# A transformer block on one core: query and key stacks filled within on-chip memory, with the work ahead of the attention loop in another order

## The reference

```python
n = layernorm(x); q, k, v = n @ Wq.T, n @ Wk.T, n @ Wv.T      # 256 x 256 each
q, k = rope(q), rope(k)                                       # halves of the 256 columns turned against each other
heads: 16 of 16
memory = elu1(k)^T v ; norm = sum(elu1(k))                    # the linear branch, per head
mem_out = elu1(q) memory / (elu1(q) norm)
attn = softmax(q k^T / 4) v                                   # per head, 1024 x 1024
x = x + (sigmoid(gate) * mem_out + (1 - sigmoid(gate)) * attn) @ Wo.T
x = x + moe(layernorm(x))       # 8 experts, hidden 688, silu(gate) * up, best 2 of 8 per token
```

## Time and profile before

| | |
|---|---|
| time, median of 3 runs | 445.03 us (442.81 to 445.61) |
| the profiled execution's own time | 448.04 us |
| its span in the profile | 446.1 us |
| busy PE / DVE / ACT / POOL | 405.4 / 267.7 / 198.2 / 98.2 us |
| mean granted clock of TensorE | 0.967 of full |
| HBM read / written | 30.05 / 18.74 MB |

### The profile page before, as it was taken

How to read it: one execution, slowest core, us unless ns; L and a number is a source line. 1 busy time by engine, 2 the same in 40 slices (tenths; PEclk the granted TensorE clock), 3 DMA queues, 4 the chain that set the end, 5 groups by cost and what they waited for, 6 DMA issues and landing times.

```text
span 446.1 us, 6508 instructions
## 1 busy us (share of the span) xinstructions
PE 405.4 (91%) x2144; PEld 202.0 (45%) x2145; DVE 267.7 (60%) x513; ACT 198.2 (44%) x349; POOL 98.2 (22%) x92
## 2 busy tenths in 40 slices
PE   0887799979999999999999799999999999999992
PEld 0526175222222232342332123577665677777771
DVE  6498899866888888779979610278233233233230
ACT  0236825756676766657656598411111111111110
POOL 6100660421011011001014220006421421212112
PEclk9998589998999999999989999999999999999997
DMA  6227674467264453203013169525422232211131
GB/s 201 106 71 141 108 176 95 121 209 240 97 206 148 162 190 113 63 1 129 0 39 138 49 232 337 160 72 186 84 37 37 40 44 37 35 36 25 24 107 24
DMA packets 24409, 48.15 MB, mean 108 GB/s; under 512 B 4448, under 2 KB 17888, under 8 KB 22528
## 3 DMA queue, kind: packets, MB, share of 16 engines
q0 software_dynamic: 7824, 30.27, 22.7%
q1 hardware_dynamic: 15984, 15.96, 14.4%
q10 hardware_dynamic: 576, 1.58, 1.1%
HBM read 30.05 MB, written 18.74 MB: 109 GB/s over the span
## 4 chain that ended last, share of the span: by engine, by line
PE 72%; DVE 12%; DMA 5%; issue 2%; ACT 2%; SPq 2%; another core or an unknown queue 2%; POOL 1%; DVEq 0%; POOLq 0%; ACTq 0%
PE psum L1227 66%; DVE mem L948 6%; PE psum L1491 2%; DMA parts_d<-mem 2%; DMA mem<-x 1%; ACT mem L778 1%; DMA mem<-mem 1%; PE psum L1351 1%; PE psum L1480 1%; SPq L432 1%; DVE mem L1013 1%; DMA out<-mem 1%; DVE mem L885 1%; POOL mem L539 1%
## 5 line engine op out<-in xcount | busy, mean ns | idle before, releaser
L1227 PE MATMUL psum<-mem 128*32 128x512 f32 (+10 forms) x1904 | 381.3, 461 | 18.6 <-DMA mem<-parts_d 2.8
L1227 PEld LDWEIGHTS psum<-mem 128*32 128x32 f32 (+4 forms) x1904 | 173.0, 134 | 205.0 <-issue 84.1
L948 DVE TENSOR_REDUCE mem<-psum 128x1 f32<-128x1024 f32 x128 | 152.1, 1219 | 33.3 <-PE psum L1227 30.3
L778 ACT ACTIVATE mem<-psum 128x512 f32<-128x512 f32 x256 | 137.3, 604 | 64.8 <-PE psum L1227 59.5
L792 ACT ACTIVATE mem<-psum 128x688 f32<-128x688 f32 x18 | 13.4, 746 | 85.6 <-PE psum L1227 79.4
L647 POOL DMA_INDIRECT sum_d<-mem x17 | 26.6, 1564 | 79.4 <-ACT mem L796 63.4
L1111 DVE COPY mem<-mem 128x3 f32<-128x3 f32 x18 | 3.0, 169 | 57.6 <-PE psum L1480 52.5
L1123 DVE COPY mem<-psum 128x512 f32<-128x512 f32 x18 | 12.5, 692 | 28.4 <-PE psum L1491 27.5
L796 ACT ACTIVATE mem<-psum,mem 128x256 f32<-128x256 f32 x18 | 8.5, 474 | 40.8 <-PE psum L1227 36.6
L599 POOL DMA_DIRECT2D mem<-gate_up x7 | 4.0, 572 | 75.8 <-DMA mem<-mem 75.8
L1115 DVE TENSOR_TENSOR mem<-mem,psum 128x688 f32<-128x688 f32 x18 | 15.7, 870 | 5.0 <-ACT mem L792 4.3
(11 more groups left out here) (121 smaller groups left out, 199.4 us busy)
## 6 DMA issues: line engine op xcount, KB each, us to landing
mem<-gate_up POOLq DMA_DIRECT2D x8, 1376.0 KB
xg_d<-mem POOLq DMA_DIRECT2D x8, 1036.0 KB, 5.9
mem<-down POOLq DMA_DIRECT2D x4, 1024.0 KB, 10.4
mem<-parts_d SPq DMA_DIRECT2D x24, 128.0 KB, 4.3
mem<-parts_d SPq DMA_DIRECT2D x48, 64.0 KB, 2.3
parts_d<-mem SPq DMA_DIRECT2D x18, 128.0 KB, 1.8
mem<-xg_d SPq DMA_DIRECT2D x16, 129.5 KB
mem<-down POOLq DMA_DIRECT2D x2, 704.0 KB, 12.6
```

The source lines that it names most:

```text
L778: nc.scalar.activation(prob[:, t % 8], psum[:, score_bank(n, t)], ACT.Exp, scale=HD ** -0.5).then_inc(exp_ready, 1)
L948: V.tensor_reduce(mx[:, par, k:k + 1], banks(2 * (k % 2), 2), AX.X, ALU.max).then_inc(max_ready, 1)
L1227: return nc.tensor.matmul(*a, **k)
```

## The change

- **Stacks from SBUF.** DRAM's `parts_d` goes. `k_group` and `q_group` copy 64 partitions (a quad of a block) straight to the 16 rows of a group, four heads wide. For this a partition's place within a quad must be r * 4 + j in place of j * 16 + r: ScalarE reorders the columns of Wk and Wq into `w_turned` ahead of the projections, and the tables of cosine and sine and the mask of the state are reordered in the constants. The linear branch runs in the new order, with the same counts.
- **SP's order.** `first_stacks(i)` for i = 0, 1, 2 issues six 64 KB copies, each group as soon as its part is there (keys in two halves of the tokens). Then stacks(1), a wait for the low parts of block 1, stacks(2), max_rows(0, 0), stacks(3), a wait for the parts of i = 3, max_rows(1, 1). `stacks` now holds its key stack too, waits until that has landed, and issues the query stack. The loop over u is written out.
- **Block 1's splits.** GpSimd does the rotations of block 1 for the queries (i = 2, 3) and the residuals and low parts of block 1; VectorE keeps the keys' rotations.
- **Order on ScalarE.** v_copy 0 and 1 go between the high parts of block 1, v_copy 2 and 3 behind the exponential of k; hi_part(3) goes behind the copies of the turned kfeat.
- **Values between scores.** Four value tiles stay ahead of the scores, the others follow steps 3, 5, 7 and 9. lin_turn moves to steps 23 to 26, lin_state to steps 31 to 34.
- **Clears.** Fills 0 to 2 are issued on GpSimd right after the first norm, ahead of all the rest; fills 3 and 4, then 5, 6, 7 and the last one stand behind gate_up 0, 1, 2 and 3, which wait for the rows of maxima of the next unit, as before.

```diff
+            def quad_rows(w, part, qd, c):
+                p = qd % 2 * 4 * HD
+                return parts[p:p + 4 * HD, w, part, qd // 2, c]
+            def k_group(g, qd, c, done):
+                sp.dma_start(kst[g * HD:(g + 1) * HD, qd, :, c], quad_rows(0, KPART[g], qd, c)).then_inc(done, 16)
+            def q_group(g, qd, hf, sl):
+                sp.dma_start(qst[g * HD:(g + 1) * HD, sl], quad_rows(1, QPART[g], qd, cols(hf))).then_inc(q_in, 16)
+            def first_stacks(i):
+                for part, ready in enumerate((hi_ready, mid_ready, lo_ready)):
+                    sp.wait_ge(ready[0], i + 1)
+                    for g in range(GROUPS):
+                        if i < 2 and KPART[g] == part:
+                            k_group(g, 0, cols(i), k0_in)
+                        if i == 2 and QPART[g] == part:
+                            q_group(g, 0, 0, 0)
...
             def stacks(qd):
+                k_stack(qd)
                 sp.wait_ge(k_in, 16 * GROUPS * qd)
                 sp.wait_ge(q_in, 16 * GROUPS * qd)
                 q_stack(qd, 0, qd)
...
-            k_stack(1, k_in)
+            for i in range(3):
+                first_stacks(i)
             stacks(1)
-            for i in range(3):
-                parts_out_1(i)
-            for i in range(3):
-                sp.wait_ge(part_out_1[i], 48)
-            k_stack(2, k_in)
+            sp.wait_ge(lo_ready[1], 3)
+            stacks(2)
             max_rows(0, 0)
-            stacks(2)
-            k_stack(3, k_in)
             stacks(3)
-            parts_out(3)
-            for s in range(3):
-                sp.wait_ge(part_out[3][s], 16)
+            sp.wait_ge(lo_ready[2], 1)
             max_rows(1, 1)
...
+            pool.wait_ge(xg_set, 1)
+            for e in range(3):
+                fill(e * T, (e + 1) * T)
+            for i in (2, 3):
+                w, hf = QK_IDX[i]
+                m = (tmp, tmp_odd)[i % 2]
+                pool.wait_ge(rope_mul, i + 1)
+                nc.gpsimd.tensor_tensor(qT[:, 1, cols(hf)], m[:, 2], m[:, 3], ALU.add).then_inc(rope_q1, 1)
+            pool.wait_ge(lo_ready[0], 2)
+            for i in range(3):
+                w, hf = QK_IDX[i]
+                pool.wait_ge(hi_ready[1], i + 1)
+                nc.gpsimd.tensor_tensor(RESID_1[i], (kT, qT)[w][:, 1, cols(hf)], parts[:, w, 0, 1, cols(hf)],
+                                        ALU.subtract).then_inc(res_ready[1], 1)
+            for i in range(3):
+                w, hf = QK_IDX[i]
+                pool.wait_ge(mid_ready[1], i + 1)
+                nc.gpsimd.tensor_tensor(parts[:, w, 2, 1, cols(hf)], RESID_1[i], parts[:, w, 1, 1, cols(hf)],
+                                        ALU.subtract).then_inc(lo_ready[1], 1)
...
+            FILLS = [(3, 4), (5,), (6,), (7,)]
+            for u in range(NQ):
+                load_gate_up(u)
+                for e in FILLS[u]:
+                    fill(e * T, (e + 1) * T)
+                if u == NQ - 1:
+                    fill(E * T, NSLOT)
+                pool.wait_ge(av_ps, 8 * u + 8)
+                stage_v(u + 2, u % 2, (u + 2) % NQ)
             load_gate_up(NQ)
...
+            for w in range(2):
+                act.wait_ge(w_in[w], 16)
+                nc.scalar.copy(w_turned[:, w].rearrange("p b (q r j) -> p (b q) j r", r=HD, j=4),
+                               wqkv[:, w].rearrange("p b (q j r) -> p (b q) j r", j=4, r=HD)).then_inc(w_turned_ready, 1)
...
-            for n in range(TT):
+            for n in range(4):
+                values(n)
...
-                if s in (17, 19, 21, 23):
-                    lin_turn((s - 17) // 4, (s - 17) // 2 % 2)
-                if s in (25, 27, 29, 31):
-                    lin_state((s - 25) // 4, (s - 25) // 2 % 2)
+                if s in (3, 5, 7, 9):
+                    values(4 + (s - 3) // 2)
+                if s in (23, 24, 25, 26):
+                    lin_turn((s - 23) // 2, (s - 23) % 2)
+                if s in (31, 32, 33, 34):
+                    lin_state((s - 31) // 2, (s - 31) % 2)
```

More of the change, by code:

```diff
@@ L129, in block_kernel @@
         qst = words(A + 8192, 4, 4, HALF, dt=BF16)
+        w_turned = words(A + 11264, 2, HB, H)
         max_ones = mem[SROWS:SROWS + 2, A:A + 2 * NQ * T]
@@ L395, in _ @@
             sp.dma_start(router, router_d).then_inc(router_in, 16)
[L397 to L415, removed]
-                for g in range(GROUPS):
-                    src = parts_d[0, KPART[g]].rearrange("(q j r) t -> q r j t", j=4, r=HD)[qd]
-                    sp.dma_start(kst[g * HD:(g + 1) * HD, qd], src).then_inc(done, 16)
@@ L426, in max_rows, with k_stack, q_stack @@
+            def k_stack(qd):
+                for g in range(GROUPS):
+                    k_group(g, qd, slice(0, T), k_in)
+            def q_stack(qd, hf, sl):
+                for g in range(GROUPS):
+                    q_group(g, qd, hf, sl)
             def max_rows(u, sl):
@@ L549, in stage_v, with fill @@
                 nc.gpsimd.tensor_copy(vst[:, sl, :, :, 0:HD], src).then_inc(v_staged, 1)
+            def fill(lo, hi):
+                pool.dma_start(xg_d[lo:hi].rearrange("(n p) h -> p n h", p=P),
+                               xn2[:, 0, 0:1].to_broadcast([P, (hi - lo) // P, ROW])).then_inc(xg_filled, 16)
+            pool.wait_ge(xg_set, 1)
[17 more added lines that the diff above has]
+                                        ALU.subtract).then_inc(lo_ready[1], 1)
             pool.wait_ge(v_ready, 4)
@@ L724, in _ @@
             for i in range(3):
-                act.wait_ge(rope_1, i + 1)
+                act.wait_ge(rope_q1, 1) if i == 2 else act.wait_ge(rope_k1, i + 1)
                 hi_part(i, 1).then_inc(hi_ready[1], 1)
-            v_copy(0)
-            v_copy(1)
+                if i:
+                    v_copy(i - 1)
             act.wait_ge(rope_mul, 4)
@@ L738, in _ @@
             nc.scalar.activation(exp_k, exp_k, ACT.Exp, scale=-1.0).then_inc(nexp_ready, 1)
-            act.wait_ge(rope_1, 4)
+            v_copy(2)
+            v_copy(3)
+            act.wait_ge(rope_0, 4)
+            act.wait_ge(rope_q1, 2)
             nc.scalar.activation(qfeat, qT, ACT.Relu).then_inc(relu_ready, 1)
@@ L785, in steps @@
                         turned_copy(hf, k)
+            act.wait_ge(lo_ready[1], 3)
             attention(act, steps)
@@ L934, in _ @@
             turns(3, 1).then_inc(rope_mul, 1)
-            other(3)
-            for i in range(3):
-                rest(i, 1)
-            for i in range(3):
-                low_part(i, 1)
             def score_side(i, t):
@@ L1247, in _, with values @@
             pe.wait_ge(w_in[2], 16)
-            pe.wait_ge(xnT_ready, 4)
-            for n in range(TT):
+            def values(n):
                 if n % 4 == 0:
```

97 lines of the change are left out of this document (29 added, 68 removed).

## The result

The changed kernel takes 439.76 us (median of 4 runs, 439.47 to 440.68), the kernel before 444.86 (4 runs, 442.81 to 445.61): ratio 0.9904, 95% interval 0.9874 to 0.9934, faster by 5.1 us. The forecast was 439.8. The profiled execution took 439.96 us, its span is 438.1, the mean granted clock 0.981.

The account below looks back on a forecast made before the run. TensorE, busy 91%, was taken to set the time in the long middle and at the end. 1.2 us at the loop's start plus 4.0 for the hole made 5.2, from a median of 445.03 to 439.8; range 435.5 to 444.5.

Parts of the forecast that it names:

- The sum: Whole kernel: 1.2 us won at the loop's start plus 4.0 from the hole, 5.2 us in all, giving 439.8 us.
- The first stacks: Before the scores: DRAM writes and their waits go, so the first score comes at 39.5, 6.2 us earlier.
- The lead, up to the turns: Scores before the first lin_turn: later value tiles cost nothing, pair 11 is done at 54.5, kfeat is ready at 54.6.
- GpSimd's new work is hidden under ScalarE: In the lead: GpSimd's rotations, residuals and low parts end near 46.4, before v_ready, with over 2 us to spare.
- The turns cost part of the win: Four lin_turns after steps 23 to 26, at half clock: VectorE idles, and 3.3 of the 6.2 us are left.
- The states cost another part: lin_state after steps 31 to 34: VectorE waits from 63.9 to 65.9 with the mask; 1.2 us reach the loop.
- Little is kept: Rival: kfeat late, so nothing won at the mask, or the hole stays in part; 2 us faster, 443, chance 0.18.
- The queue of SP: Before the loop: stacks(2) goes ahead of max_rows(0,0); at 131 GB/s SP is free with 6 us of slack.
- the slower rival: On-chip copies below 60 GB/s make SP block the maxima; at 50 GB/s the kernel takes 455 us; chance 0.08.
- The hole in the loop: Unit 1's rows of maxima: with no fills beside them TensorE's 2.27 us wait goes, plus 1.7 of half-rate clock, 4.0.

Follow-up runs that it names:

- its one essential part alone: The kernel before with only its stacks filled directly from SBUF in SP's new order, all else as before: 442.62 us, ratio 0.9859.
- the last experiment: The changed kernel with GpSimd's first scatter moved behind its wait for the last scores: 452.94 us against 444.16 for the kernel before, ratio 1.0204.

## Why the prediction was right

**The sum.** 5.2 us were forecast, 1.2 at the start and 4.0 for the hole, and 5.1 measured on the first chip. The traces give 0.14 and 4.04 to these terms, 4.2 us. That the total came within 0.1 us is in part luck: the kernel before had late waits in its trace which no term names, and the changed one had none. On the third chip the same kernel gained 2.5 us (0.9925, 0.99 to 0.9949). This interval overlaps that of 0.9904, but the forecast's ratio, 0.988, lies outside it; why it was 2.5 and not 4.2 stays open, as the kernel before has no trace there.

**The first stacks: right.** The first score waits for TensorE's values; the first maximum came at 40.48 against 40.2, pair 11 was done at 54.50 against 54.5. The start as a whole stood 0.54 us later: the first rotation began at 21.25 and not 20.71, because the clock rose at 18.80 and not 17.76 and the projections ahead of it ran longer at half rate. VectorE's last multiplication ended at 39.88 and not at 38.2 (0.54 of it from there, 1.07 from L898 beside GpSimd): with 0.60 us of idle time ahead of the first maximum it was near to deciding.

**The lead, up to the turns: chain right, one hand-over missed.** kfeat was forecast at 54.6 and came at 55.66. The step "GpSimd's new work is hidden under ScalarE" failed: two of ScalarE's three middle parts wait 0.50 us each for a residual of GpSimd's 1.13, so exp_k's first half started at 45.14 and not about 43.7 (0.4 of it is the later start). The prediction compared when GpSimd's work ends, and not its pace with ScalarE's. GpSimd's operations were sized rightly (L556 and L561, 3.39 for three, 1.13 each). The copies of the weights take 2.04 us for the two and not 1.2, and still hide: TensorE's second eight transposes start at 14.48, where they started at 14.42.

**The turns cost part of the win: right, and slightly larger.** VectorE idles 4.08 and 0.75 us, 3.8 were forecast; the clock was at half there, 49.52 to 59.76. The rows of maxima are sent at 64.72 against 63.9.

**The states cost another part: the mechanism was right, the size too large by 1.1.** The mask begins at 66.83 against 65.9; it was given 1.2 us to win, and the loop starts 0.14 earlier. Some 0.5 of the shortfall is the clock's rise at the start, the rest kfeat. The prediction's own bound, nothing won if kfeat comes 1.2 us later than worked out, and the rival *Little is kept* (kfeat late, nothing at the mask) named this case: kfeat came 1.06 later, and for the start of the loop it is what happened. The experiments turn the account round. Of the 6.3 us of the first maximum, 3 buy nothing, as a score 3 us later gives the same start; the others are worth some 2 at the loop, and kfeat, 2.8 us later than before (55.66 against 52.85), takes these back. I had kfeat ahead of the first turn, at 1.7 us later than before, but did not follow that all else ahead of it is slack then, and that a microsecond of kfeat is then nearly one of the loop's start (1.7 for 2.0).

**The queue of SP: right, with less to spare.** Key stack 1 ran at 114 GB/s with the DMA engines full. The windows of the changed kernel, 39 to 44 and 52 to 56 us (length, busy engines, clock, DMA share, GB/s):

```profile
39.00:44.00 5.00, 4.98 (x23) 3.33 (x23) 4.40 (x6) 3.46 (x4) 4.04 (x4) 0.97 0.94 114
52.00:56.00 4.00, 1.33 (x5) 0.42 (x5) 2.50 (x3) 3.47 (x2) 4.00 (x2) 0.50 0.98 112
```

This is under the 131 of the reads from DRAM, far over the 60 from which the slower rival decides, and SP issued the rows within 0.1 us of their being ready. It had stood 3.6 us for them, where 6 were forecast. The Trainium skill ("SBUF — State Buffer", Door 1: The DMA port swizzle) gives about 109 GB/s for 16 partitions; 112 and 114 lie near it. A source in SBUF at the same time took nothing off that figure, though it may be part of the step down from 131: no run separates them.

**The hole in the loop: size right, cause only half.** 4.0 forecast, 4.04 found between first exponential and first turn, with no half-rate stretch behind. (The rows were needed 23.1 us after the loop's start, 97.0 less 73.92, and not 23.4; nothing hangs on it.) But I gave it to the clears' move. The runs show that the direct stacks alone remove it as well, and that in the kernel before the fills stood at 89.05 because of the writes of parts. My step looked at what ran beside the rows and not at why it ran just then.

## What to carry to other kernels

When several edits feed one start, find which input arrives last there and delay each other input by a few microseconds: an input that can be 3 us later for nothing is not worth an edit. Run a large change also as its one essential part alone: here that part was faster than the whole, because the reordering around it lengthened the chain that set the start. Check a match of forecast and median term by term in the traces: here the total agreed to 0.1 us and one of its two terms was off by 1.1. Before a transfer is moved out of another's way, ask why it was issued at that moment.

## What the runs showed of the hardware

- **GpSimd against small VectorE operations.** Two-input VectorE operations on SBUF stood until a GpSimd one ended: 1.76 us and not 0.69 beside L551, 2.05 and not 0.17 beside L582. The Trainium skill ("SBUF — State Buffer", 🔬 SBUF: two separate sides) calls the shared port pair an exclusive lock also for VectorE operations with two SBUF inputs, against a GpSimd operation that reads SBUF; these rows agree. It goes both ways: L551 at 34.57 took 1.64 us, and 1.27 at 39.96; beside the first, VectorE's L914 ran until 35.08. The cast of 16 columns with one input took 0.40 and not 0.17. Not every such pair is held: two comparisons of 32 columns at 295.23 took 0.29 us beside a GpSimd power of 4 columns.
- **Issues of on-chip copies.** Six from SBUF to SBUF take SP 3.78 us, 0.63 each, the six reads from DRAM took 2.68, 0.45 each.
- **A copy that reorders columns on ScalarE** (128x512, stride of 4) takes 1.02 us from SBUF to SBUF; a plain one out of PSUM takes 0.59, a plain cast within SBUF 0.62.
- **Late waits that depend on the chip or the execution.** The trace of the changed kernel on the third chip, 240 to 252 us:

```profile
247.05 2.23 ACT L784 ACTIVATE mem<-psum 128x512 f32<-128x512 f32 x4 [3.46 <-remote]
247.13 1.22 DVE L949 TENSOR_REDUCE mem<-psum 128x1 f32<-128x1024 f32 x1 [2.27 <-remote]
247.70 4.67 PE L1228 MATMUL psum<-mem 98*128 98x512 bf16 x16 [2.62 <-ACT mem L784]
```

 TensorE loses 2.62 us here, and the clock is at half rate from 248.72 to 252.13. Eleven of the fourteen traces (before, the changed kernel and twelve experiments) have such a wait between 241 and 251 us, twelve have the one of 6.1 to 6.2 us between 310 and 318. The first trace of the changed kernel and that of the last experiment have neither. From unit 5 to 6 it is 23.0 us in this trace and 19.0 in the first of the same kernel, which is as large as the differences between the ratios. The comparisons of start and hole above therefore stop at the first turn of a unit's output. What releases these waits stays open.
